# One unrolled block from the second combine to the gated layer, with other batches' stages among the heads of the masked attention

## The chip, the cores and the metric

One core of a Trainium2 chip. The metric is the device time of one execution in microseconds. Engines are named as in the profile: PE (TensorE), DVE (VectorE), ACT (ScalarE), POOL (GpSimd), SP (SyncE, which here only issues transfers).

## The reference

Two layers over x (4 batches x 512 tokens x 256), with a context of the same shape. What matters here is the second half:

```
x = x + attention_0(layernorm(x), ctx)            # 16 heads of 16, causal, relative positions
x = x + experts_0(layernorm(x))                   # 2 of 8 experts per token; the kernel's "combine" adds both
x = x + attention_1(layernorm(x), ctx, mask) @ Wo # 16 heads of 16, masked
x = x + bitlinear(silu(bitlinear(x, gate)) * bitlinear(x, up), down)
# bitlinear: each token's row scaled to +-127 and rounded, weights rounded to -1, 0, 1
```

## The kernel before, in words

A tile is 128 tokens; a batch has NI = 4 tiles, and there are 16 tiles and 64 pairs of batch and head. The kernel is a chain of blocks. In each one every engine has its own instruction stream, written out by hand; the streams meet at semaphores only, and the end of a block is a meeting of all of them. The blocks are: opening (projections), causal attention of layer 0 (unrolled), routing, the expert tiles, and then the four that the change touches:

- **combine** (L1557 ff.). For each batch SP loads the two experts' rows of its tokens (L1570, into `got`), DVE adds them to x, weighted (L1588, 8 operations a batch), takes statistics (L103), and runs the layer norm: `norm` on DVE (L111 to L125) with one square root on ACT (`root`, L149), scaling on ACT (`apply`, L143). PE turns the rows (L156), ACT copies them (L163), PE multiplies with Wq (`product`, L197, two half batches), ACT copies twice (L214, L215), and DVE splits the result in three bf16 pieces (`split`, L221 to L226), from which an f32 product is later made in one bf16 matmul over 96 rows. SP stores the pieces to DRAM (`store`, L238) and at the end waits for all of them.
- **masked_attention** (L663 ff.). A software pipeline over the 64 heads; a loop of 8 steps runs most of them (`run_heads`). At step n SP loads head n+3 (L360), PE scores head n+2 (L717) by four row blocks i, DVE takes each block's row maximum under the mask (L784, which is also what frees the bank), POOL negates the four maxima and splits them in three pieces (L758 to L766), one step later PE turns them (L731) and ACT copies them beside the head's operands (L815), so that for head n PE computes scores minus maximum, turned (L722), with the mask added by a second matmul (L724), and ACT exponentiates (L811). PE weighs the values, four heads at a time, one key block per step (`weigh`, L404); every fourth step their outputs are copied, turned and divided (`copy_out` L411, `turn` L417, `divide` L424, L426). Two banks hold scores, two the turned scores: PE waits before row block i until DVE (or ACT) has finished block i - 2. The ternary weights of the gated layer are prepared on DVE among the first and the last heads (L1653, L1673 to L1679).
- **closing** (L1002 ff.), for all batches in one pipeline: DVE copies the heads into rows of tokens (L1032), PE turns them (L1100), ACT copies (L1120), PE projects with Wo (L1107), DVE adds to x (L1041), the norm again, the largest magnitude per token (L1053), POOL scales and rounds (L1078), ACT makes bf16 integers (L1125), PE turns (L1090), ACT copies (L1129).
- **ffn** (L1682 ff.), per tile: gate and up products (L1767, L1772, two banks each), Silu on ACT (L1820), product on DVE (L1731), its maximum (L1733) and four scales (L1735 to L1740), rounding on POOL (L1751), integers on ACT (L1812), transposes (L1781), copy (L1807), down product (L1789), scaling and sum on DVE (L1717), output by SP (L1757).

```
for n in range(first, ROUND):                     # run_heads, L335: the order of every engine
    step(n, n % ROUND, n // ROUND)
...
wait(pe, s_soft, NI * m + i - 1)                  # before L717: DVE is at most two blocks behind
wait(pe, s_exp, NI * m + i - 1)                   # before L722: the same for ACT
pe.wait_ge(s_mp, 5 * (m + 1))                     # before L731: POOL's pieces of the maxima
```

## Time and profile before

| | us |
|---|---|
| median of 3 runs (1203.1 to 1204.17) | 1203.2 |
| the profiled execution, its own time | 1203.75 |
| its span | 1202.0 |
| combine (735 to 793) | 58 |
| masked attention (793 to 1087) | 294 |
| closing and gated layer (1087 to 1202) | 115 |

A span is the time from the first to the last instruction. "Busy" counts time in which an engine executes; an engine that waits for a semaphore is idle, and the profile names what released it. A granted clock of 1.00 stands for TensorE's full 2.4 GHz.

### The profile page before, as it was taken

To read this page: it belongs to the slowest core of one execution; us is meant where nothing else is said; L and a number is where in the kernel's file an instruction comes from. 1 tells how busy PE (TensorE), PEld (TensorE's weight loads), DVE (VectorE), ACT (ScalarE), POOL (GpSimd) and SP (SyncE) were. 2 spreads that over 40 slices of the span, in tenths; PEclk is the share of its full clock that TensorE was granted. 3 is DMA by queue.
4 is the path that set the end of the run, shared out by engine and by line. 5 is a ranking of instruction groups with operands and counts; after the bars stand their busy time and mean duration, and the time that the engine had idled before them with its cause. 6 is when DMAs were issued, how large, how long until landed. Compare 5 with 4: busy or idle time off the path is not lost. (4 is left out here: it accounts for less than half of the span.)

```text
span 1202.0 us, 21977 instructions
## 1 busy us (share of the span) xinstructions
PE 1050.5 (87%) x6945; PEld 658.6 (55%) x6979; DVE 659.1 (55%) x1993; ACT 636.5 (53%) x1275; POOL 200.0 (17%) x466
## 2 busy tenths in 40 slices
PE   7999999999978698999999991648999999987487
PEld 5555555655545498999999981213333333325254
DVE  4427888888856611211111104857666666775697
ACT  2447877877633232333333321526777777763697
POOL 0000000000000122222222210012222222330222
PEclk9958999999999898999999995869999999998798
DMA  5087898888749336666666644443111111100001
GB/s 184 1 306 293 321 330 322 316 321 324 290 141 360 136 110 226 223 222 219 225 218 222 220 140 153 152 147 91 47 49 46 47 46 46 47 20 10 0 32 40
DMA packets 75342, 199.55 MB, mean 166 GB/s; under 512 B 7880, under 2 KB 40904, under 8 KB 69256
## 3 DMA queue, kind: packets, MB, share of 16 engines
q1 hardware_dynamic: 71528, 188.45, 46.1%
q0 software_dynamic: 3744, 10.23, 2.2%
q8 instruction: 36, 0.59, 0.2%
q14 instruction: 34, 0.28, 0.1%
HBM read 134.82 MB, written 63.83 MB: 165 GB/s over the span
## 5 line engine op out<-in xcount | busy, mean ns | idle before, releaser
L784 DVE CUSTOM_DVE_ANT_0 unused<-mpsS,mask_bias 128x512 bf16<-128x512 f32 x256 | 172.0, 691 | 83.3 <-PE mpsS L717 82.9
L1526 ACT ACTIVATE hT<-ph,w 128x128 f32<-128x128 f32 x312 | 89.2, 369 | 207.7 <-PE ph L1500 207.7
L811 ACT ACTIVATE mPT<-mpsB 128x512 f32<-128x512 f32 x256 | 152.7, 597 | 81.1 <-PE mpsB L724 67.1
L1500 PE MATMUL ph<-xT,w 128*128 128x128 f32 x1248 | 152.1, 282 | 7.5 <-DMA w<-in_w1p 7.1
L1500 PEld LDWEIGHTS ph<-xT,w 128*128 128x128 f32 x1248 | 147.3, 197 | 10.8 <-issue 10.5
L1545 DVE TENSOR_TENSOR xn<-py,b 128x256 f32<-128x256 f32 x39 | 16.6, 425 | 247.4 <-PE py L1510 247.4
L1510 PE MATMUL py<-w,hT 128*128 x624 | 141.2, 379 | 0.7 <-DVE xn L1545 0.7
L659 ACT ACTIVATE scores<-scores,nm 128x512 f32<-128x512 f32 (+3 forms) x256 | 125.6, 557 | 9.8 <-DVE nm L624 9.8
L1510 PEld LDWEIGHTS py<-w,hT 128*128 128x128 f32 x624 | 115.6, 190 | 15.2 <-issue 1.1
L717 PE MATMUL mpsS<-mqk 96*128 96x512 bf16 x256 | 101.2, 397 | 19.5 <-DMA mqk<-packed 15.7
L611 DVE CUSTOM_DVE_ANT_0 scores<-psS,bias 128x512 f32<-128x512 f32 (+3 forms) x176 | 77.8, 487 | 54.6 <-PE psS L552 38.2
L618 DVE COPY PT<-psT 128x1024 f32<-128x1024 f32 (+1 forms) x96 | 100.2, 1044 | 7.2 <-PE psT L568 7.1
L722 PE MATMUL mpsB<-mqk 99*128 99x512 bf16 x256 | 98.9, 386 | 0.3 <-ACT mPT L811 0.2
L568 PE MATMUL psT<-ident,scores 128*128 128x128 f32 x640 | 89.7, 280 | 10.1 <-DVE PT L618 10.1
L724 PE MATMUL mpsB<-maskT,identb 128*128 128x512 bf16 x230 | 88.5, 385 | 0.0
L568 PEld LDWEIGHTS psT<-ident,scores 128*128 128x128 f32 x640 | 69.8, 143 | 18.6 <-DVE PT L618 16.8
L650 ACT COPY stage<-psE 128x1024 f32<-128x1024 f32 (+1 forms) x62 | 54.2, 874 | 46.9 <-PE psE L536 45.9
L1474 POOL DMA_INDIRECT pair_out<-xn,dst_row x39 | 42.5, 1089 | 213.7 <-DVE xn L1545 213.7
L717 PEld LDWEIGHTS mpsS<-mqk 96*128 96x128 bf16 x256 | 24.9, 98 | 85.4 <-DVE mmx L784 36.0
L404 PE MATMUL psOm<-mPT,spreadm 128*32 128x512 f32 x512 | 67.8, 604 | 1.2 <-ACT headsm L411 0.8
L390 POOL TENSOR_TENSOR spreada<-V,zerosa 128x272 f32<-128x272 f32 x16 | 11.6, 724 | 325.0 <-PE psOa L404 267.2
L546 PE MATMUL psS<-xnT,xn 16*128 16x512 f32 (+3 forms) x256 | 62.6, 508 | 0.5 <-DVE mx L611 0.5
(267 smaller groups left out, 1621.5 us busy)
## 6 DMA issues: line engine op xcount, KB each, us to landing
w<-in_w1p SPq DMA_DIRECT2D x39, 1028.0 KB, 5.8
rel<-stage SPq DMA_DIRECT2D x44, 640.0 KB, 4.6
bias<-rel SPq DMA_DIRECT2D x44, 640.0 KB, 7.1
x<-rel SPq DMA_DIRECT2D x20, 640.0 KB, 6.8
mqk<-packed SPq DMA_DIRECT2D x64, 192.0 KB
w<-in_w2p SPq DMA_DIRECT2D x8, 1024.0 KB, 12.7
rel<-x SPq DMA_DIRECT2D x10, 640.0 KB, 3.2
rel<-mask_bias SPq DMA_DIRECT2D x10, 640.0 KB, 5.0
```

The source lines that it names most:

```text
L568: tr = nc.tensor.transpose(psT[:, h, to:to + P], scores[p % 3][:, h, at:at + P], ident[:, :])
L611: ttr = nc.vector.tensor_tensor_reduce(out=scores[soft % 3][:, h, at:at + w], in0=psS[:, h, off:off + w], in1=bias[soft % 3][:, h, at:at + ...
L618: nc.vector.tensor_copy(PT[late % 4][:, :, 512 * u:512 * u + WU[u]], psT[:, :, 0:WU[u]]).then_inc(s_tev, 1)
L659: ex = nc.scalar.activation(to, to, ACT.Exp, bias=nm[:, soft % 3, h, i:i + 1], scale=1.0 / 4)
L717: nc.tensor.matmul(psS[i % 2][:, :], qk[slot][0:KP, i * P:(i + 1) * P], qk[slot][0:KP, S:2 * S], start=True, stop=True).then_inc(s_smm, 1)
L722: nc.tensor.matmul(psB[i % 2][:, :], qk[slot][:, S + i * P:S + (i + 1) * P], qk[slot][:, 0:S], start=True, stop=False)
L724: nc.tensor.matmul(psB[i % 2][:, :], identb[:, :], maskT[:, i, :], start=False, stop=True).then_inc(s_bmm, 1)
L784: nc.vector.tensor_tensor_reduce(out=unused[:, i, :], in0=psS[i % 2][:, :], in1=mask_bias[:, i, :], scale=1.0, scalar=-3.0e38, op0=ALU.add ...
L811: nc.scalar.activation(PT[r][:, j, :], psB[j % 2][:, :], ACT.Exp, scale=1.0 / 4).then_inc(s_exp, 1)
L1500: mm = nc.tensor.matmul(ph[half][:, q * P:(q + 1) * P], w1[i][:, dk * F + f * P:dk * F + (f + 1) * P], xT[i][:, dk, :], start=(dk == 0), s ...
L1510: mm = nc.tensor.matmul(py[:, 0:D], hT[i][:, f, :], w2[:, bass.ds(e, 1), f * D:(f + 1) * D].rearrange("p a d -> p (a d)"), start=(f == 0), ...
L1526: g = nc.scalar.activation(hT[i][:, f, :], ph[half][:, q * P:(q + 1) * P], ACT.Gelu, bias=w1[i][:, DK * F + f:DK * F + f + 1])
```

## The change

The four blocks become two: `masked_layer` (which holds combine of all batches, all 64 heads, and closing and gated layer of batches 0 to 2) and `final_batch` (closing and gated layer of batch 3). `PieceProjection`, `combine`, `run_heads`, `TernaryWeights`, `closing` and `ffn` go. All loops over heads are unrolled. Every engine walks over the same steps n = -16 ... 72 with four slots i each, and a few functions say what else is in a slot:

```diff
+            CLOSE, FFN = 23, 28
+            EARLY = B - 1
...
+                def combine_at(n):
+                    b, at = n // HEADS + 1, n % HEADS
+                    return (b, at) if b < B else (None, None)
+                def closing_at(n, i):
+                    c, at = divmod(NI * (n - CLOSE) + i, NI * HEADS)
+                    return (c, at) if 0 <= c < EARLY else (None, None)
+                def ffn_at(n, i):
+                    c, at = divmod(NI * (n - FFN) + i, NI * HEADS)
+                    if not 0 <= c < EARLY or at >= 5 * ROUND:
+                        return None, None, None
+                    t, k = divmod(at, ROUND)
+                    now = NI * c + t if t < NI else None
+                    return now, (NI * c + t - 1 if t > 0 else None), k
+                def weight_at(n, i):
+                    w, at = divmod(n - 2, 6)
+                    return (w, NI * at + i) if 0 <= w < 3 else (None, None)
```

So combine of batch b + 1 begins with the first head of batch b (batch 0 in the 16 steps before any head, where nothing else runs), closing of batch c at step 23 + 16 c, a tile of its gated layer every two steps from 28 + 16 c on. SP:

```diff
+                    for n in range(FIRST, last + 1):
+                        b, at = combine_at(n)
+                        if b is not None and at in (9, 10):
+                            store_queries(b, at - 9)
+                        if at == 4 and b + 1 < B:
+                            load_pairs(b + 1)
+                        if n in (-3, -2):
+                            load_weight(n + 3)
+                        if n == 7:
+                            load_weight(2)
+                        if h := head_at(n, LOAD):
+                            m, slot, turn = h
+                            if m % ROUND == 0:
+                                sp.wait_ge(s_qout[m % HEADS // ROUND], 3 * 16 * (m // HEADS + 1))
+                            wait(sp, s_bmm, NI * (m - RING + 1))
+                            load_head(sp, m, qk[slot][0:KP, :], s_qk[slot])
```

PE, behind the row block of each slot. All added products share two banks: `psU`, and `psX`, in which the heads' outputs are turned too. `u_free` and `x_free` name the semaphore that frees them:

```diff
+                            if b is not None and (at, i) in ((6, 0), (6, 2)):
...
+                                rows_turned(b, i // 2)
+                                u_free = s_tcev, DK * b + i // 2 + 1
+                            if b is not None and (at, i) in ((7, 0), (8, 2)):
+                                pe.wait_ge(*u_free)
+                                queries(b, at - 7)
+                                u_free = s_qf, DK * b + at - 7 + 1
...
+                            if c is not None and at in (0, 2):
...
+                                heads_turned(c, at // 2)
+                            if c is not None and at in (4, 6):
+                                pe.wait_ge(*x_free)
+                                projected(c, at // 2 - 2)
+                                x_free = s_res, 2 * c + at // 2 - 1
+                            if c is not None and at == 18:
+                                pe.wait_ge(*u_free)
+                                tokens_turned(c)
...
+                            if now is not None and k in (0, 4):
+                                pe.wait_ge(*u_free)
+                                wide(psU, 0, now, k // 4, s_g)
+                                u_free = s_a, 2 * now + k // 4 + 1
+                            if now is not None and k in (1, 5):
+                                pe.wait_ge(*x_free)
+                                wide(psX, 1, now, k // 4, s_u)
+                                x_free = s_h, 2 * now + k // 4 + 1
+                            if prev is not None and k == 2:
+                                pe.wait_ge(*u_free)
+                                hidden_turned(prev)
+                                u_free = s_he, prev + 1
+                            if prev is not None and k == 7:
+                                pe.wait_ge(*x_free)
+                                down(prev)
+                                x_free = s_y, prev + 1
```

The other engines follow the same table. DVE, behind the maximum of its slot: statistics of combine at step 3, the norm at (4, 0); in closing the sums at 5 and 7, statistics at 8 and 9, the norm at 10, the largest magnitude at 13, six scales at 14; in a tile's eight slots gate times (tanh + 1) at 1 and 5, hidden product at 2 and 6, maximum at 6, scales at 7, the previous tile's result at the next 0. ACT: in combine of batches 1 to 3 the eight weightings of `got` (steps 0 and 1), in a tile tanh at 0 and 4, integers of the previous tile at 1, its copy at 2. POOL: in combine of batches 1 to 3 the eight additions (steps 1 and 2), the scaling (step 5) and the splits (steps 7 to 9); in closing scaling (11, 12) and rounding (15, 16); in a tile the previous tile's rounding at 0. In a step POOL's negation of the maxima stands behind all of these.

Two computations change form. The norm has no square root on ACT any more, but a bit trick and three Newton steps on DVE (13 small operations):

```diff
+                nc.vector.tensor_scalar(self.sd[:, :].bitcast(I32), self.ve[:, :].bitcast(I32), -0.5, self.SEED,
+                                        ALU.mult, ALU.add).then_inc(self.s_rs, 1)
+                for k in range(self.ROUNDS):
...
+                    nc.vector.tensor_tensor(self.t1[:, :], self.sd[:, :], self.sd[:, :], ALU.mult).then_inc(self.s_rs, 1)
+                    nc.vector.tensor_tensor(self.t2[:, :], self.t1[:, :], self.half[:, :], ALU.mult).then_inc(self.s_rs, 1)
+                    nc.vector.scalar_tensor_tensor(out=self.sd[:, :], in0=self.t2[:, :], scalar=1.5, in1=self.sd[:, :],
+                                                   op0=ALU.add, op1=ALU.mult).then_inc(self.s_rs, 1)
```

And in batches 0 to 2 Silu is made from Tanh, while `final_batch` keeps Silu:

```diff
+                        nc.scalar.activation(hid[T % 2][:, half * S:(half + 1) * S], psU[:, :], ACT.Tanh,
+                                             scale=gh[:, T % NI:T % NI + 1]).then_inc(s_th, 1)
...
+                        nc.vector.scalar_tensor_tensor(out=part, in0=part, scalar=1.0, in1=psU[:, :],
+                                                       op0=ALU.add, op1=ALU.mult).then_inc(s_a, 1)
```

Smaller: `divide` writes the heads' outputs straight as rows of tokens, so the copies L1032 go; the query product is copied once by ACT and its first piece made by DVE or POOL; the query's buffers are single (`full`, `left`); the ternary weights are prepared in steps 2 to 19, in the room of the context (`ctxT`), no longer partly at the end. `final_batch` does closing for 4 tiles with the norm, the scaling and the rounding on DVE, and the gated layer for 4 tiles as before with two banks each.

## Rows read from the trace of the kernel before

**Rows 1.** Windows by stage: us, each engine's busy time (instructions), granted clock, DMA share, GB/s.

```profile
core 0 of [0], span 1202.0 us
...
56.00:360.00 304.00, 287.32 (x2498) 172.70 (x2499) 221.33 (x681) 209.47 (x400) 11.58 (x16) 0.93 0.80 293
...
735.00:793.00 58.00, 24.31 (x64) 11.70 (x64) 43.85 (x125) 21.44 (x44) 0.00 (x0) 0.71 0.52 171
793.00:1070.00 277.00, 264.49 (x1488) 92.09 (x1514) 191.73 (x545) 190.99 (x324) 79.33 (x331) 0.97 0.20 56
...
1087.00:1134.00 47.00, 24.82 (x128) 20.38 (x128) 29.10 (x130) 25.33 (x49) 7.73 (x16) 0.79 0.02 6
1134.00:1202.00 68.00, 54.29 (x377) 31.52 (x384) 55.37 (x129) 53.17 (x65) 17.95 (x16) 0.93 0.09 32
```

**Rows 2.** Timeline of one masked head: start, us, engine, line, operation, out<-in, [idle before <-releaser].

```profile
903.62 0.39 PE L717 MATMUL mpsS<-mqk 96*128 96x512 bf16 x1
...
903.85 0.38 PE L722 MATMUL mpsB<-mqk 99*128 99x512 bf16 x1
...
905.03 0.39 PE L731 MATMUL mpsM<-identb,mpieces 128*3 128x128 bf16 x4
...
906.58 0.69 DVE L784 CUSTOM_DVE_ANT_0 unused<-mpsS,mask_bias 128x512 bf16<-128x512 f32 x1
...
906.76 1.07 PE L404 MATMUL psOm<-mPT,spreadm 128*32 128x512 f32 x8
...
907.76 0.39 PE L717 MATMUL mpsS<-mqk 96*128 96x512 bf16 x1
...
908.75 0.21 POOL L766 TENSOR_TENSOR mpieces<-mrest,mpieces 128x4 bf16<-128x4 f32 x1
```

**Rows 3.** Timeline of TensorE, the weighting of the 31st head after the one above.

```profile
1038.89 1.07 PE L404 MATMUL psOm<-mPT,spreadm 128*32 128x512 f32 x8
```

**Rows 4.** Timeline from the first combine to the first masked matmul.

```profile
735.46 1.00 DVE L1588 SCALAR_TENSOR_TENSOR x<-got,prob,x 128x256 f32<-128x256 f32 x2 [15.79 <-DMA got<-pair_out]
...
742.19 0.16 DVE L121 TENSOR_TENSOR t2c<-t1c,vec 128x4 f32<-128x4 f32 x1
...
747.75 5.82 PE L197 MATMUL prpscq<-xnT,wcq 128*128 128x512 f32 x8 [0.67 <-ACT xnT L163]
...
788.30 3.18 SPq L360 DMA_DIRECT2D mqk<-packed  x4
...
793.04 1.01 PE L717 MATMUL mpsS<-mqk 96*128 96x512 bf16 x2 [12.50 <-DMA mqk<-packed]
```

**Rows 5.** Timeline, the weighting of the last masked head.

```profile
1078.95 1.06 PE L404 MATMUL psOm<-mPT,spreadm 128*32 128x512 f32 x8
```

**Rows 6.** Timeline of combine and closing: matmuls at the high clock.

```profile
756.25 3.67 PE L197 MATMUL prpscq<-xnT,wcq 128*128 128x512 f32 x8 [1.80 <-ACT piecescq L215]
...
771.53 1.09 PE L156 MATMUL lnpsc<-ident,xn 128*128 128x128 f32 x8 [4.42 <-ACT xn L143]
...
1100.21 3.72 PE L1107 MATMUL opo<-wo,aT 128*128 128x256 f32 x16 [0.72 <-ACT aT L1120]
```

**Rows 7.** Groups by line: busy us, mean ns | idle before, releaser.

```profile
L1733 DVE TENSOR_REDUCE ha<-hh 128x1 f32<-128x1024 f32 x16 | 19.5, 1220 | 0.6
...
L1812 ACT ACTIVATE hq<-hr,minus_magic 128x1024 bf16<-128x1024 f32 x16 | 18.4, 1148 | 2.5 <-POOL hr L1751 2.5
...
L1807 ACT COPY hqT<-ptx 128x1024 bf16<-128x1024 bf16 x16 | 16.2, 1012 | 5.7 <-PE ptx L1781 5.7
...
L811 ACT ACT_TABLE_LOAD x1 | 1.3, 1283 | 0.0
```

**Rows 8.** One line's instructions: min/median/max ns, first and last start.

```profile
L1751 POOL TENSOR_SCALAR hr<-hh,hs x16: 1122/1122/1124, 1140.5 to 1193.1; 128x1024 f32<-128x1024 f32 x16
```

**Rows 9.** Timeline of TensorE around a wait for a head's load.

```profile
811.90 0.39 PE L717 MATMUL mpsS<-mqk 96*128 96x512 bf16 x1 [1.95 <-DMA mqk<-packed]
...
813.69 0.61 PE L717 MATMUL mpsS<-mqk 96*128 96x512 bf16 x1
```

More of the change, by code:

```diff
@@ L685, in masked_attention @@
                 psM = ctx.enter_context(nc.psum_tensor("mpsM", [P, 1024], BF16))
+                psU = banks(ctx, "mpsU", 1)[0]
+                psX = vals.psX
+                psUb = psU[:, :].bitcast(BF16)
                 s_qk = [sem(f"s_mqk{r}") for r in range(RING)]
-                names = ("one", "smm", "soft", "mp", "mt", "row", "bmm", "exp", "seen")
-                s_seen_p = sem("s_mseenp")
-                s_one, s_smm, s_soft, s_mp, s_mt, s_row, s_bmm, s_exp, s_seen = (sem(f"s_m{n}") for n in names)
@@ L690, in masked_attention @@
-                block = ctx.enter_context(nc.Block())
+                names = ("one", "smm", "soft", "mp", "mt", "row", "bmm", "exp", "seen", "seenp", "const")
+                s_one, s_smm, s_soft, s_mp, s_mt, s_row, s_bmm, s_exp, s_seen, s_seen_p, s_cst = (sem(f"s_m{n}") for n in names)
+                names = ("gm", "x", "tc", "tcev", "qm", "qf", "split", "wqr", "wo")
+                s_gm, s_x, s_tc, s_tcev, s_qm, s_qf, s_split, s_wqr, s_wo = (sem(f"s_c{n}") for n in names)
+                s_got = [sem(f"s_got{b}") for b in range(B)]
@@ new lines, in queries, with total @@
+                    def queries(b, eh):
+                        pe.wait_ge(s_wqr, 16)
+                        pe.wait_ge(s_tcev, DK * (b + 1))
+                        for dk in range(DK):
+                            mm = nc.tensor.matmul(psU[:, :], wqr[:, dk, eh * P:(eh + 1) * P], xnTb[:, dk, :],
+                                                  start=(dk == 0), stop=(dk == DK - 1))
+                        mm.then_inc(s_qm, 1)
+                    def total(w):
+                        pe.wait_ge(s_cst, 2)
+                        pe.wait_ge(s_sum, w + 1)
+                        nc.tensor.matmul(psU[:, 0:1], ones[:, :], asum[:, w:w + 1], start=True, stop=True).then_inc(s_wt, 1)
@@ L713, in step @@
+                    pe.wait_ge(s_one, RING)
+                    u_free = x_free = None
+                    for n in range(FIRST, last + 1):
+                        soft, rows, late = (head_at(n, k) for k in (SOFT, ROWS, 0))
                         for i in range(NI):
                             if soft:
-                                m, slot, turn = soft
-                                wait(pe, s_soft, NI * m + i - 1)
-                                nc.tensor.matmul(psS[i % 2][:, :], qk[slot][0:KP, i * P:(i + 1) * P], qk[slot][0:KP, S:2 * S],
-                                                 start=True, stop=True).then_inc(s_smm, 1)
+                                score(soft, i)
@@ new lines, in hidden_integers, with hidden_out @@
+                    def hidden_integers(T):
+                        act.wait_ge(s_hr, T + 1)
+                        wait(act, s_ht, T)
+                        nc.scalar.activation(hq[:, :], hid[T % 2], ACT.Identity, bias=minus_magic[:, :]).then_inc(s_hq, 1)
+                    def hidden_out(T):
+                        act.wait_ge(s_ht, T + 1)
+                        wait(act, s_dn, T)
+                        nc.scalar.copy(hqT[:, :], psUb[:, :]).then_inc(s_he, 1)
+                    for n in range(FIRST, last + 1):
+                        if n % GROUP == 0 and (h := group_at(n, 2)):
@@ L988, in build @@
                             mask_bias, maskT)
+            wq = [sb(ctx, f"wq{n}", [P, 2 * F], BF16) for n in range(3)]
+            ws = sb(ctx, "ws", [P, 3])
             with nc.cleanup_on_exit():
[L990 to L995 removed]
```

1169 lines of the change are left out of this document (630 added, 539 removed).

## The prediction

> **What bounds the kernel now.** I read the split by stage first, then one head of the masked attention in order of time, then the seams on both sides of that stage.
>
> By stage [rows 1]: combine fills 58 us with TensorE busy for 24 of them, the masked heads 277 us with TensorE busy for 264, closing 47 us with 25, the gated layer 68 us with 54. The change puts three quarters of the half-empty stages among the heads of the full one. So the question is what the full one can still take.
>
> One head [rows 2]: the scoring matmul of its first row block starts at 903.62, the maxima of the next head in line are turned at 905.03, weighting starts at 906.76, and the following head's first matmul at 907.76, 4.14 us later. Every fourth head also turns its outputs; the average is (1038.89 - 906.76) / 31 = 4.26 us [rows 2, 3]. TensorE has no real gap in it: 12 matmuls of 512 columns, one every 0.22 us (903.62 to 903.85), four small transposes, and 1.0 us of weighting. VectorE ends its four maxima at 907.27 and pauses about 1.1 us until the next head's. But POOL then splits the maxima in five small steps, the last of them to 908.96, and TensorE needs them 1.41 us into the next head, at 909.17: a late fourth maximum is late on TensorE by nearly as much. **There is slack on VectorE and ScalarE as a sum, and almost none in the order of the steps.**
>
> **The change, part by part.**
>
> *Front seam.* Now the first masked matmul stands at 793.04 and the first combine at 735.46 [rows 4]. New, combine of batch 0 alone runs ahead: 8 multiply-adds of 0.5 (4 us), statistics 1.4, the normalization 2.7 (four aggregates 0.4, then 12 small operations of 0.16 as at 742.19, 0.2 with the handover), scaling 1.5: 745. Turning and copying in one bank, half by half, 4: 749. Each query product costs half of 5.82 at the low clock [rows 4], 0.6 of copy and 2.3 of splitting before the next copy may start: 759. The store, head 0's load (from 788.30 to 793.04 it takes 4.7 today) and a 1 MB weight load that SP issues ahead of it: about 768, bounds 762 and 773. **Gain 25 us.**
>
> *Back seam.* Today the last head's weighting ends at 1080.0 [rows 5] and the span at 1202.0 [rows 1]: 122 us. New: (a) The gated layer of batch 2 occupies steps 60 to 69, but the last head is step 63; its last two tiles have no heads beside them. With one bank of each kind a tile is a chain: rounding 1.12, integers 1.15, transposes 0.6, copy 1.01, gate matmul and tanh and product 2.1, the last half's product 0.7, maximum 1.22, scales 0.8 and the handovers [rows 7, 8], 9.3 us, where today a tile takes (1193.1 - 1140.5) / 15 = 3.5 [rows 8]. Two tiles and the last one's way out: 29 us. (b) The final block: closing for one batch, nothing overlapped: turns 2, projection 5.5 cold (3.72 warm [rows 6]), sum, statistics and norm 4, scaling, maxima, rounding, integers, turning 8: 19.5. Then four tiles: 68 - 12 x 3.5 = 26 [rows 1, 8], less 1 for the drain already in it: 25. Sum (a) + (b) 73.5, bounds 68 and 82. **Gain 48.5 us.**
>
> *TensorE work moved among the heads*, per batch, warm: turning for the queries 1.09, query products 3.67 [rows 6]; turning the heads 1.1, projection 3.72, tokens 0.5; four tiles of 8 x 0.22 + 0.5 + 0.9 = 3.1 each. Three batches of the first five (30 us), and ten tiles (31; two run behind the heads). TensorE is full, so all of it lengthens the stage: **+60 us.** With these three terms alone the sum would be 1203.75 - 25 - 48.5 + 60 = 1190.
>
> *New waits inside the steps.* Each engine's order is fixed, TensorE may be only two row blocks ahead of VectorE (L784) and ScalarE (L811), and psU and psX are single banks.
> - The norm (2.7 us) stands in one slot on VectorE behind the first maximum, in front of the second. TensorE's fourth block needs the second: instead of at 2.4 us it starts at 4.5. Wait 2.1, three times in combine. With ScalarE's eight extra multiplications (1.0), the splits ahead of POOL's negation (0.6) and smaller ones: 3.9 per combine, and 2.5 once where the combine of batch 3 meets the gated layer of batch 0. Together 14.
> - In closing the norm stands behind the third maximum, so the fourth, POOL's negation and the turned maxima are late (2.4). Then the largest magnitude (1.2) and six scales (1.2) in adjacent slots push the fourth maximum and POOL again (2.6); integers (1.1) and the turning of the tokens wait for POOL's rounding, which queues behind the negation (1.2); the collision with the query product in psU 0.5. Sum 6.7, three times: 20.
> - A tile of the gated layer: ScalarE's integers wait for POOL's rounding (1.12), which queues behind the negation, and TensorE's transposes wait for them: 1.2 us. The down product waits for the last product on VectorE: 0.5. So 1.8 for each of the eight tiles fully beside heads: 14.
> - Transfers: the pair loads (1 MB) and the query stores (768 KB per half batch, two) stand on SP's queue ahead of head loads that are prefetched by about one step. Today a head load in such company left TensorE idle 1.95 us before 811.90 [rows 9]. Nine such meetings against three now, some covered by the longer steps: 8.
>
> The sum is 56. Counted singly, waits that fall into one step are partly counted twice, so I take **46**, bounds 0 (the engines catch up in the weighting microsecond) and 75.
>
> *At no cost:* the weights' three magnitudes and nine roundings on VectorE run among heads today and stay there, only earlier; the masked stage pays them either way. Dividing straight into rows of tokens saves VectorE's copies of the heads, which stood beside the closing's first transposes. Unrolled code instead of a loop costs nothing: the causal block is unrolled already, and TensorE is busy for 287 of its 304 us [rows 1]; if that cover fell, it would be a wait before steps, which I leave in the upper bound. The square root on ScalarE goes (its place is taken by the small steps priced above).
>
> Sum: 1203.75 (the profiled execution: its span of 1202.0 and 1.75 around it; the median of the runs, 1203.2, is 0.5 below) - 25 - 48.5 + 60 + 46 = **1236 us**.
>
> **Rivals.**
>
> *Covered (ends faster).* The place is VectorE's pause after the fourth maximum and the microsecond of weighting: if those absorb the bursts, the waits cost at most 10 us and the time is about 1197. For: VectorE was busy 192 of 277 us and ScalarE 191 [rows 1], and the moved work raises a head with a gated tile to only about 5.3 on VectorE against 5.7 on TensorE. Against: the maxima's way over POOL has next to no slack [rows 2]. It decides at waits of 13 us in sum. Chance 0.17.
>
> *The clock falls.* After the idle 1.95 us the matmuls from 813.69 on take 0.61 instead of 0.39, the lower of the two levels (1.2 against 2.4 GHz), for about 3 us [rows 9]. Closing makes several waits of 1 to 2.4 us per batch, the tail more. If a dozen of them cost 1.7 us each, the time is 1256. Against: the masked stage as a whole was granted 0.97 [rows 1]. Chance 0.15. The Trainium skill, TensorE: Matmul & The Clock Gate, section A second HAM failure mode: psum-queue depth-cycling, says that short idles between groups which cycle through accumulation banks make the clock swing; by it this rival would be the forecast.
>
> *Tables.* The new gate uses Tanh between Exp. Every change of function set costs a load of 1283 ns on ScalarE [rows 7]. Two loads for each of the 24 gates are 61 us, 5.1 per tile, on an engine whose own work fills most of a tile's two steps: some 50 us come on top, 1286. The profile can't tell whether Tanh shares Exp's set. Chance 0.03. The Trainium skill, ScalarE: Activation LUTs, section Table sets: the hidden batching unit, lists tanh in exp's set, and the chance goes by that.
>
> **How the numbers follow.** Forecast 0.60, its own range 1214 to 1252 (waits 24 to 62); covered 0.17; clock 0.15; tables 0.03; 0.05 for anything in between that ends within 0.2% (2.4 us, about what a measurement of this kernel can tell from no change). The range 1197 to 1258 takes in the covered case and the clock, and leaves out the tables and the tails. Faster 0.17, same 0.05, slower 0.78.
>
> **What would show it.** The first masked matmul about 25 us earlier. Heads alone still 4.1 to 4.6; a pair of heads with a gated tile about 13 us instead of 8.5; between steps CLOSE + 2 and FFN about 19 us instead of 13. TensorE's idle time released by VectorE's maxima, by POOL's pieces and by ScalarE's integers. No wave of table loads. From the last head's weighting to the end 73 us. Wrong, if gated pairs take under 12 us and closing steps under 5 each: then the covered case holds; or if heads without added work have become longer, which would be the code or the loads.

## The result, and the profile after

The changed kernel takes 1248.4 us (median of 4 runs, 1246.3 to 1250.6) against 1203.35 for the kernel before in the same session: ratio 1.037, 95% interval 1.035 to 1.040. It is 3.7% slower. The profiled execution took 1249.97 us, its span is 1247.9.

Line numbers are now those of the changed kernel: L748 scores, L756 and L758 score again with keys and queries exchanged, L1004 takes VectorE's maxima, L938 to L946 are POOL's negation and pieces, L766 turns them, L1203 the exponentials, L341 the weighting. "Step n" with a time is the stretch from the weighting of step n - 1 to that of step n. Two rows of the split by stage:

```profile
core 0: us, PE busy (x) PEld busy (x) DVE busy (x) ACT busy (x) POOL busy (x), PEclk, DMA share, GB/s
769.10:802.60 33.50, 24.51 (x96) 7.38 (x100) 25.14 (x77) 18.92 (x34) 13.07 (x40) 0.81 0.27 86
802.60:1171.40 368.80, 320.60 (x1798) 127.14 (x1832) 250.18 (x723) 230.64 (x387) 146.82 (x389) 0.96 0.17 52
```

The second is the stretch from the weighting of step 4 to that of step 63. In the kernel before the same 59 steps ran from 824.61 to 1078.95 [rows 5], 254.3 us; the weighting of its step 4 and its split of that stretch:

```profile
824.61 1.06 PE L404 MATMUL psOm<-mPT,spreadm 128*32 128x512 f32 x8
...
824.60:1079.00 254.40, 247.09 (x1443) 86.45 (x1470) 177.77 (x499) 181.76 (x310) 74.54 (x304) 1.00 0.16 44
```

So the heads became 114.6 us longer: TensorE is busy 73.5 us more (320.6 against 247.1) and idle 41 us more (48.2 against 7.3), and the granted clock is 0.96 where it was 1.00. Three differences make up the whole:

| | before | after | difference |
|---|---|---|---|
| start to weighting of step 4 | 824.6 | 802.6 | -22.0 |
| step 4 to step 63 | 254.3 | 368.9 | +114.6 |
| step 63 to the end | 123.1 | 76.5 | -46.6 |

Both seams gave back nearly what was forecast. The first masked matmul, which stood at 793.04 [rows 4], stands here (timeline of the front):

```profile
756.84 4.61 SPq L713 DMA_DIRECT2D packed<-pieces  x6
761.49 0.68 SPq L706 DMA_DIRECT2D ctxT<-in_gateT  x1
762.21 0.87 SPq L299 DMA_DIRECT2D mqk<-packed  x1
...
769.11 1.04 PE L748 MATMUL mpsS<-mqk 96*128 96x512 bf16 x2 [12.63 <-DMA mqk<-packed]
```

The loss is inside the heads. The weightings of steps 22 to 27, across the first closing, and of steps 29 to 31, the first with two tiles of the gated layer under way, against 4.26 us a step on average before [rows 2, 3]:

```profile
897.94 1.07 PE L341 MATMUL psOm<-mPT,spreadm 128*32 128x512 f32 x8
905.57 1.06 PE L341 MATMUL psOm<-mPT,spreadm 128*32 128x512 f32 x8
914.87 1.06 PE L341 MATMUL psOm<-mPT,spreadm 128*32 128x512 f32 x8
919.21 1.06 PE L341 MATMUL psOm<-mPT,spreadm 128*32 128x512 f32 x8
930.06 1.41 PE L341 MATMUL psOm<-mPT,spreadm 128*32 128x512 f32 x8
936.77 1.07 PE L341 MATMUL psOm<-mPT,spreadm 128*32 128x512 f32 x8
...
946.77 1.07 PE L341 MATMUL psOm<-mPT,spreadm 128*32 128x512 f32 x8
954.67 1.06 PE L341 MATMUL psOm<-mPT,spreadm 128*32 128x512 f32 x8
961.18 1.07 PE L341 MATMUL psOm<-mPT,spreadm 128*32 128x512 f32 x8
```

Steps 23 and 24 (7.6 and 9.3 us) hold the turned heads, the projection and both query products, in the timeline four groups of 1.9 us: TensorE's own work. Step 26 takes 10.85 us and has hardly any of it. Its timeline, from the closing's normalization on:

```profile
919.58 0.38 DVE L276 BATCH_NORM_AGGREGATE mvd<-statsd 128x2 f32<-128x6 f32 x4
...
922.13 0.69 DVE L1004 CUSTOM_DVE_ANT_0 unused<-mpsS,mask_bias 128x512 bf16<-128x512 f32 x1
922.24 2.42 POOL L295 TENSOR_SCALAR xn<-x,mvd,sdd 128x256 f32<-128x256 f32 x2 [2.29 <-DVE sdd L290]
...
922.89 0.39 PE L748 MATMUL mpsS<-mqk 96*128 96x512 bf16 x1 [2.08 <-DVE mmx L1004]
...
925.93 2.42 POOL L295 TENSOR_SCALAR xn<-x,mvd,sdd 128x256 f32<-128x256 f32 x2
926.02 0.58 PE L766 MATMUL mpsM<-identb,mpieces 128*3 128x128 bf16 x4 [2.30 <-POOL mpieces L946]
926.53 0.61 PE L748 MATMUL mpsS<-mqk 96*128 96x512 bf16 x1
...
928.39 1.22 DVE L1038 TENSOR_REDUCE am<-xn 128x4 f32<-128x1024 f32 x1 [4.03 <-POOL xn L295]
929.52 0.68 DVE L1004 CUSTOM_DVE_ANT_0 unused<-mpsS,mask_bias 128x512 bf16<-128x512 f32 x1
```

Here the reader sees the chain: the norm holds a maximum back (TensorE idle 2.08 us), POOL scales two tiles before it splits the maxima (TensorE idle 2.30 us), and VectorE then stands 4.03 us in front of the largest magnitude until POOL has scaled the other two, with the step's fourth maximum queued behind it. Behind the two idles of TensorE its matmuls last 0.61 instead of 0.38 us. Steps 25 to 27 in one row:

```profile
914.87:936.77 21.90, 15.93 (x85) 5.58 (x85) 14.38 (x55) 10.16 (x17) 12.50 (x26) 0.84 0.20 64
```

The same three steps took 12.90 us before, TensorE busy for 12.84 of them at a clock of 1.00. So of the 9.0 us more, 5.9 are idle time of TensorE, and 3.1 are busy time, at a granted clock of 0.84. Over all heads the view of waits gives (TensorE's largest, and VectorE's of this kind):

```profile
PE mpsM L766 <- POOL mpieces L946: 14.8, 15, 2.3
DVE am L1038 <- POOL xn L295: 12.1, 3, 4.0
PE mpsU L827 <- ACT ctxT L1186: 9.9, 9, 1.9
PE mpsS L748 <- DVE mmx L1004: 9.7, 10, 2.2
```

### The profile page after: what moved, and what is told of

It is laid out like the page before. It is cut to its first block and busy times, and to the rows that moved or that the text cites. A ratio compares the mean times of both kernels' runs of the same rounds, so it can differ in the third digit from the quotient of the medians.

```text
span 1247.9 us, 20848 instructions
## 1 busy us (share of the span) xinstructions
PE 1065.7 (85%) x6943; PEld 657.5 (53%) x6983; DVE 660.3 (53%) x2006; ACT 616.3 (49%) x1240; POOL 259.8 (21%) x534
## 5 line engine op out<-in xcount | busy, mean ns | idle before, releaser
L1004 DVE CUSTOM_DVE_ANT_0 unused<-mpsS,mask_bias 128x512 bf16<-128x512 f32 x256 | 173.9, 689 | 114.2 <-PE mpsS L748 112.6
L1203 ACT ACTIVATE mPT<-mpsB 128x512 f32<-128x512 f32 x256 | 152.5, 597 | 119.7 <-PE mpsB L758 104.8
L748 PE MATMUL mpsS<-mqk 96*128 96x512 bf16 x256 | 103.0, 405 | 28.6 <-DMA mqk<-packed 14.3
L756 PE MATMUL mpsB<-mqk 99*128 99x512 bf16 x256 | 101.3, 396 | 1.6 <-ACT mqk L1207 1.0
L1915 POOL DMA_INDIRECT pair_out<-xn,dst_row x39 | 42.4, 1087 | 212.5 <-DVE xn L1986 212.5
L758 PE MATMUL mpsB<-maskT,identb 128*128 128x512 bf16 x220 | 86.6, 394 | 0.0
L748 PEld LDWEIGHTS mpsS<-mqk 96*128 96x128 bf16 x256 | 25.1, 99 | 109.7 <-issue 53.4
L587 ACT COPY stage<-psE 128x1024 f32<-128x1024 f32 (+1 forms) x62 | 54.1, 872 | 46.5 <-PE psE L473 45.5
L341 PE MATMUL psOm<-mPT,spreadm 128*32 128x512 f32 x512 | 72.4, 638 | 0.4
```

What stands on the lines that cost most here:

```text
L748: nc.tensor.matmul(psS[i % 2][:, :], qk[slot][0:KP, i * P:(i + 1) * P], qk[slot][0:KP, S:2 * S], start=True, stop=True).then_inc(s_smm, 1)
L756: nc.tensor.matmul(psB[i % 2][:, :], qk[slot][:, S + i * P:S + (i + 1) * P], qk[slot][:, 0:S], start=True, stop=False)
L758: nc.tensor.matmul(psB[i % 2][:, :], identb[:, :], maskT[:, i, :], start=False, stop=True).then_inc(s_bmm, 1)
L1004: nc.vector.tensor_tensor_reduce(out=unused[:, i, :], in0=psS[i % 2][:, :], in1=mask_bias[:, i, :], scale=1.0, scalar=-3.0e38, op0=ALU.add ...
L1203: nc.scalar.activation(PT[n % ROUND][:, j, :], psB[j % 2][:, :], ACT.Exp, scale=1.0 / 4).then_inc(s_exp, 1)
```

## The experiments

Ratios are to the kernel before, timed beside each run. Its median there lay between 1204.5 and 1206.8 us, against 1203.35 beside the change, so rows are best compared by their ratios. "Heads" is the stretch from the weighting of step 4 to that of step 63, "tail" from there to the end of the span, both from the one profiled execution of each. The first masked matmul stands between 766.5 and 772.1 us in runs that hardly differ up to there, so a difference of 2 us in front of the heads says nothing.

| kernel | median us | ratio, 95% interval | heads | tail |
|---|---|---|---|---|
| before | 1203.35 | | 254.3 | 123.1 |
| the change | 1248.4 | 1.037, 1.035 to 1.040 | 368.9 | 76.5 |
| e_shift | 1243.5 | 1.032, 1.028 to 1.036 | 365.0 | 73.1 |
| e_thin | 1251.1 | 1.038, 1.035 to 1.041 | 365.6 | 75.9 |
| e_early2 | 1233.3 | 1.022, 1.019 to 1.025 | 348.5 | 80.7 |
| e_early0 | 1210.3 | 1.004, 1.002 to 1.005 | 283.2 | 123.1 |
| e_order | 1242.5 | 1.032, 1.029 to 1.036 | 364.8 | 73.6 |
| e_turn | 1265.9 | 1.051, 1.048 to 1.054 | 383.3 | 73.5 |
| e_turn2 | 1247.9 | 1.036, 1.033 to 1.038 | 366.4 | 74.6 |
| e_order0 | 1203.0 | 0.999, 0.996 to 1.001 | 276.7 | 124.1 |
| e_both2 | 1235.1 | 1.024, 1.020 to 1.029 | 350.3 | 80.6 |
| e_lay2 | 1217.9 | 1.012, 1.010 to 1.014 | 332.7 | 80.6 |
| e_tern0 | 1207.8 | 1.003, 1.001 to 1.004 | 281.3 | 123.4 |
| e_late0 | 1196.5 | 0.993, 0.991 to 0.995 | 275.2 | 124.3 |

**e_shift: POOL's scaling in another form.**

```
-  ns.tensor_scalar(xn[:, t, :], x[:, t, :], self.mv[:, j, 0:1], self.sd[:, j:j + 1], ALU.subtract, ALU.mult)
+  ns.tensor_scalar(xn[:, t, :], x[:, t, :], self.sd[:, j:j + 1], self.shift[:, j:j + 1], ALU.mult, ALU.add)
```

> The changed kernel with one edit: the scaling of the normalization (the second LayerNorm's and the combine's) multiplies by 1/sigma and adds a shift, as the rounding does, in place of subtracting the mean and multiplying; VectorE computes the shift in one more small operation per batch. Theory A (POOL's scaling is slow because of its form: 1.21 to 1.30 us for 128x256 against 0.47 for the rounding of the same size, and VectorE and then the fourth maximum wait up to 4.0 us for four of them): the scaling falls to about 0.5 us, each closing loses about 3 us, each combine among heads about 2, the small operation gives 1 back: 1234 us, between 1229 and 1239. Rival B (POOL is slow there because VectorE works beside it, or because of two scalar pointers): the scaling stays above 1.1 us and the time is within 2 us of 1248. Rival C (the scaling gets faster, but steps are bound by something else in the closing): scaling 0.5 us and time above 1243.

The groups of POOL, the change first, then this run:

```profile
L295 POOL TENSOR_SCALAR xn<-x,mvc,sdc 128x256 f32<-128x256 f32 x12 | 15.5, 1304 | 0.1
L295 POOL TENSOR_SCALAR xn<-x,mvd,sdd 128x256 f32<-128x256 f32 x12 | 14.5, 1218 | 9.9 <-DVE sdd L290 9.9
```

```profile
L298 POOL TENSOR_SCALAR xn<-x,sdc,shiftc 128x256 f32<-128x256 f32 x12 | 7.5, 639 | 0.1
L298 POOL TENSOR_SCALAR xn<-x,sdd,shiftd 128x256 f32<-128x256 f32 x12 | 6.5, 553 | 10.5 <-DVE shiftd L293 10.5
```

The form is what made it slow: 0.55 us instead of 1.22 with two scalar pointers in both. But by the ratios the time fell by about 6 us, not 14, and the first closing's steps 26 and 27 only from 10.85 and 6.71 to 9.7 and 6.3. Theory A holds for the operation; for the time neither A's range (1229 to 1239) nor B's was met, and 1243.5 lies just inside C's. The scaling was one link of the chain.

**e_thin: less TensorE work in the gated layer** (half a contraction of gate and up, one of eight blocks of the down product).

```
-  for dk in range(DK):      (gate, up)        -  for f in range(FB):      (down)
+  for dk in range(1):                         +  for f in range(1):
```

> The changed kernel with part of TensorE's work among the heads left out: of the gate and up products only the first half of the contraction (one matmul of 512 columns instead of two), of the down product one of its eight blocks. What is computed for batches 0 to 2 is therefore wrong in the gated layer; order, waits, transfers and all other engines stay. Left out per tile: 4 x 0.22 + 7 x 0.11 = 1.65 us of TensorE at the high clock, ten tiles beside heads, two behind them. Theory A (the folded gated layer costs both TensorE's work and waits around it, about half of the omitted work is hidden by waits for POOL, ScalarE and VectorE): 9 us less, 1239, between 1234 and 1243. Rival B (TensorE's sum of work is the bound): 17 to 20 us less, 1229 to 1231. Rival C (a chain of waits alone sets the step): within 3 us of 1248.

Four tiles beside heads, the change first, then this run:

```profile
946.77:1002.60 55.83, 46.87 (x283) 18.73 (x288) 43.87 (x126) 39.66 (x67) 24.01 (x58) 0.97 0.13 37
```

```profile
949.03:1004.89 55.86, 43.69 (x244) 15.75 (x248) 42.58 (x124) 39.09 (x66) 23.31 (x58) 0.94 0.12 36
```

TensorE is busy 3.2 us less and the stretch is as long as before. (The 3.2 is less than the 6.6 left out; the granted clock fell from 0.97 to 0.94 beside it.) The tiles of the second batch, which have no combine beside them, say the same more cleanly: from the weighting of step 45 to that of step 53 TensorE is busy 45.5 us in the change and 41.6 here, and the stretch takes 52.2 and 51.9. That is rival C: in steps full of gated work the time does not hang on TensorE's sum. The 3 us that the heads lost lie in the two steps of each batch that hold its first tile's gate and up products and nothing else (28, 29, 44, 45, 60, 61: 5.0 us each, here 4.6) and in step 63 (5.4 and 4.6). The ratio did not change.

**e_early2 and e_early0: fewer batches among the heads.** The late batches run in two blocks written like those of the kernel before.

```
-  EARLY = B - 1                                  +  EARLY = 2        (0)
-  final_batch(identb, wq, ws)                    +  late_batches(identb, wq, ws, EARLY)
```

> The changed kernel with projection and gated layer of batches 0 and 1 among the heads (EARLY = 2 instead of 3), and those of batches 2 and 3 behind the heads in two blocks that work like the ones of the kernel before (two banks of each kind, several tiles under way). Combine stays folded as in the change. Theory A (every folded batch costs more than it saves; the last one most, since it ends in a tail): the closing steps of batch 2 (13.5 us extra) and the gated tiles of the last four heads (6) go, and the part from the last head to the end falls from 75 to about 69: 1223 us, between 1216 and 1230. Rival B (folding the early batches is free or better, only the tail of batch 2 is at fault): 1216 or less, and unfolding more batches loses time again. Rival C (folding pays per batch, the combine or the unrolled code is at fault): above 1240.

> As the kernel with EARLY = 2, but no batch's projection and gated layer run among heads (EARLY = 0): all four run behind them in pipelined blocks as in the kernel before. What is left of the change is the combine of batches 1 to 3 among the heads, the weights' loading and rounding at its new places, and the unrolled code. Theory A (the closing and gated layer among heads are what costs; the combine is about even, 24 us gained ahead of the heads against 14 of TensorE's work and about 12 of waits): 1201 us, between 1195 and 1207. Rival B (only the tail is at fault): higher than with EARLY = 2. Rival C (combine among heads or unrolled code at fault): above 1212.

Heads and tail give the price of each part. Combine alone (e_early0): heads +28.9 against before, the stretch ahead of them -21.2, tail level: 7.7 us lost by the spans, 4.4 by the medians of its session. The first two projections and gated layers: heads +65.3, tail -42.4: 23 lost, 11.5 each. The third: +20.4 and -4.2: 16 lost. So theory A's direction holds: every folded batch loses (rival B would have had e_early2 lowest). Both numbers came out 9 to 10 us high, outside their ranges. For e_early2 the heads fell as expected (20.4 for 19.5), but the tail rose from 76.5 to 80.7 where it was to fall by 6: the change's tail is a good one. For e_early0 the combine took 28.9 among heads instead of 26 and gave back 21 instead of 24. Its steps without any added work (29 to 32) take 4.1 to 4.6 us, as in the kernel before, so unrolling by itself costs nothing there.

**e_order: the same work in other slots.**

```
-  if b is not None and (at, i) == (4, 0):  lnc.norm(dve, b)
+  if b is not None and (at, i) == (4, 3):  lnc.norm(dve, b)
-  at == 10: lnd.norm    at == 13: largest    at == 14: token_scales    (POOL at 11, 12, 15, 16)
+  at == 11: lnd.norm    at == 15: largest, token_scales                (POOL at 12, 13, 16, 17)
```

> The changed kernel with the same work in other slots: the normalization of the combine goes from behind the first maximum of its step to behind the fourth, that of the closing from behind the third maximum to behind the fourth; POOL's four scalings follow one row block later; the largest magnitude and the token scales, which stood in front of the fourth maximum of step CLOSE+3, go behind it; rounding, integers and turned tokens follow one row block later. No instruction is added or taken away. Theory A (the bursts cost because a maximum is queued behind them, and POOL's pieces and TensorE behind that; behind the fourth maximum they fall into VectorE's pause and the weighting): the step of the combine's normalization loses 2.1 us, the steps CLOSE+2 to CLOSE+4 together 5 to 6 us, three times each: 1227 us, between 1221 and 1234. Rival B (the engines' sums of work are too large, a burst costs wherever it stands): within 4 us of 1248. Rival C (the scaling on POOL, 1.2 us each, is what is waited for, and it keeps its place between two heads' pieces): between 1236 and 1244.

The time, 1242.5, lies in rival C's range and above theory A's. Step 20, with the norm of batch 2's combine, fell from 6.9 to 4.2 us, as theory A has it; the first of the three (first masked matmul to the weighting of step 6) fell from 47.0 to 44.2, and step 36, where the third meets a gated tile, from 8.1 to 7.0. The closing gained little: step 26 fell to 6.2, step 27 rose from 6.7 to 9.1. Timeline of that place:

```profile
916.97 4.84 POOL L295 TENSOR_SCALAR xn<-x,mvd,sdd 128x256 f32<-128x256 f32 x4 [1.01 <-DVE sdd L290]
...
921.85 1.22 DVE L1038 TENSOR_REDUCE am<-xn 128x4 f32<-128x1024 f32 x1 [1.52 <-POOL xn L295]
```

Four slow scalings in a row (4.84 us) now hold the negation and the largest magnitude, and the scales come on top of it. Most of the wait was moved by one step. That suggests that the two cures belong together, which e_order0, e_both2 and e_lay2 try.

**e_turn and e_turn2: the transposes of the hidden tile later.** e_turn moves ScalarE's integers too, e_turn2 leaves them.

```
 e_turn:   integers k == 1 -> 2,   transposes and copy k == 2 -> 3
 e_turn2:  integers k == 1,        transposes and copy k == 2 -> 3
```

> The changed kernel, and in a tile of the gated layer ScalarE's integers, TensorE's transposes and ScalarE's copy of them stand one row block later, so that TensorE comes to the transposes about 1.5 us later than now, when ScalarE's integers are further on (now it idles 0.8 to 1.9 us there). Nothing is added or taken away. Theory A (this wait is a good part of what a tile costs, which the halved matmuls showed not to be TensorE's work): a tile's pair of heads falls from 13.0 to about 12.0, 1238 us, between 1232 and 1243. Rival B (the wait only moves, to the second gate product behind the copy in the same bank): within 4 us of 1248. Rival C: slower by 4 or more, since the copy now stands in front of the second gate product.

> The changed kernel; in a tile of the gated layer ScalarE's integers keep their place (second row block), and only TensorE's transposes and ScalarE's copy of them go one row block later, in front of a head's weighting. Theory A (TensorE waits 0.8 to 1.9 us for the integers because it comes too early; in the run that moved both, the integers stood behind ScalarE's row copy, so the wait stayed and the copy came on top): the wait goes, the copy lies beside the weighting, a pair of heads falls from 13.0 to about 12: 12 tiles, 1236 us, between 1230 and 1242. Rival B (the wait is not the bound of a tile, the second gate product's or the down product's wait takes its place): within 3 us of 1248. Rival C (like the last run, the copy delays the exponentials behind it): 1252 or more.

In e_turn the wait stayed, since the integers now stand behind the step's row copy on ScalarE:

```profile
1065.25 0.58 ACT L1207 COPY mqk<-mpsM 3x512 bf16<-3x512 bf16 x1
1065.86 1.15 ACT L1186 ACTIVATE ctxT<-ctxT,minus_magic 128x1024 bf16<-128x1024 f32 x1
...
1067.15 0.61 PE L827 MATMUL mpsU<-identb,ctxT 128*128 128x128 bf16 x8 [1.90 <-ACT ctxT L1186]
```

By the ratios it cost 16 us. In e_turn2 the wait is nearly gone, and the time stays within noise (waits of TensorE over four tiles, the change first, then e_turn2):

```profile
PE mpsU L827 <- ACT ctxT L1186: 4.9, 4, 1.9
PE mpsS L748 <- DVE mmx L1004: 0.7, 1, 0.7
```

```profile
PE mpsS L748 <- DVE mmx L1004: 3.2, 1, 3.2
...
PE mpsU L827 <- ACT ctxT L1186: 0.9, 2, 0.5
```

That is rival B: beside a combine, other waits took its place. In the second batch's four tiles, which have no combine beside them, the wait fell from 4.0 to 1.3 us with no other in its place, and the weightings of steps 45 to 53 came 50.3 instead of 52.2 us apart. So the longest wait in a view is not by itself the price of its removal: here 1.9 us of time came of 2.7 us of waits in one place, and 0.4 us of 4.0 in the other (55.4 instead of 55.8 for steps 30 to 37).

**e_order0 and e_both2: the two cures together**, without and with gated layers among heads (e_both2 with e_turn's move).

> The kernel with EARLY = 0 (combine alone among heads), the combine's normalization behind the fourth maximum, and the scaling as a multiplication and an addition. Theory A (a combine's 9.6 us among heads are 4.8 of TensorE's work and 4.8 of waits, 2.1 of them at the normalization, 0.5 to 1 at the scaling): 8 us less than the 1210 of EARLY = 0, 1202, between 1199 and 1205, so about level with the kernel before. Rival B (bursts cost wherever they stand): 1207 to 1211.

> The kernel with EARLY = 2, with the three edits together: normalizations and largest magnitude behind the fourth maximum, scaling as a multiplication and an addition, transposes of the hidden tile one row block later. By theory A: 1233 less 6 (combine) less 11 (two closings) less 8 (eight tiles) less 2: 1206, between 1199 and 1214. If it is under 1200, folding pays once the steps are laid well; rival B (sums of work): above 1225.

e_order0 is level with the kernel before; the heads lost 6.5 us against e_early0, where 8 were expected. e_both2 missed by 29 us. Its trace says where: the eight tiles (steps 30 to 37 and 46 to 53) take 116.9 us against 108.0 in e_early2, where 8 less were expected, which is 17 of the 29 and has the sign of what e_turn's move did alone; the two closings gained 3 us (steps 25 to 28 of each) where 11 were expected.

**e_lay2: two batches folded, everything in its place.** Over e_both2: transposes and integers of the hidden tile as in e_turn2, token scales behind the next fourth maximum, rounding, integers, turned tokens and the gated layer after them, and the roundings of the weights behind the fourth maximum.

> EARLY = 2 with everything laid by the theory: normalizations and largest magnitude behind the fourth maximum, token scales behind the next fourth maximum (and what follows them later, the gated layer two steps later), scaling as multiplication and addition, integers kept and transposes one row block later, the weights' roundings on VectorE behind the fourth maximum. Theory A (a folded batch costs TensorE 17.7 us and gives back 21; all above that is waits made by the order): 1233 less 8 (combine) less 5 to 6 per closing less 1.2 per tile less 3 for the weights: 1201, between 1195 and 1212. Rival B (waits move elsewhere): 1220 to 1230.

1218, not 1201; it lies between the ranges of theory A and of rival B. The closing is mended: the weightings of steps 24 to 27,

```profile
913.78 1.07 PE L344 MATMUL psOm<-mPT,spreadm 128*32 128x512 f32 x8
918.12 1.07 PE L344 MATMUL psOm<-mPT,spreadm 128*32 128x512 f32 x8
924.49 1.06 PE L344 MATMUL psOm<-mPT,spreadm 128*32 128x512 f32 x8
928.63 1.07 PE L344 MATMUL psOm<-mPT,spreadm 128*32 128x512 f32 x8
```

take 14.85 us where the change took 21.9 and heads alone take 12.9. The same three steps took 19.7 with the order alone (e_order), 20.3 with the form alone (e_shift) and 18.2 with both (e_both2), so the rest came with the token scales and what follows them. TensorE idles 1.7 us of the 14.85 instead of 6.0, and the granted clock is 1.00 instead of 0.84. (It was 1.00 in e_order's three steps too, with 5.8 us idle but no single wait above 1.9; what exactly lowers it is not settled here.) Some of the work was only moved back by a step or two, but from the weighting of step 22 to that of step 29, which holds all of the closing in both, it is still 40.8 against 48.8 us, of which about 1 is a gate and an up product that now come later. That shows the theory for the closing: the waits came of the order and of one slow operation. The gated layer is not mended (steps 46 to 55 of this run take 61.7 us, steps 44 to 53 of the change 62.2, of the kernel before 42.3), and the weights' new place costs some us, 4.6 by the next run. Folding the two batches well still costs 332.7 - 281.3 = 51.4 us among heads (both with the weights at that place) and gives back 42.8 in the tail.

**e_tern0: the weights' roundings behind the fourth maximum.**

```
-  if w is not None and at in (2 * NI + 1, 3 * NI + 1, 4 * NI + 1):  ternary(...)
+  if w is not None and at in (2 * NI + 3, 3 * NI + 3, 4 * NI + 3):  ternary(...)
```

> EARLY = 0 with normalization behind the fourth maximum, scaling as multiplication and addition, and the nine roundings of the weights (1.36 us each on VectorE) behind the fourth maximum instead of behind the second. Theory A (a burst between two maxima delays the maxima behind it by nearly its length less VectorE's slack): steps 4 to 18 fall by 0.3 us each where a rounding stands: 3 us less than the run before it, 1200, ratio to the kernel before 0.994 to 0.998. Rival B (the roundings were covered): the same as that run, 0.9986.

Slower than e_order0 by 4.6 us of heads, against both theories. Two places make up 3.4 of it. The first of each weight's passes now stands in the slot of the first combine's norm, directly behind it:

```profile
804.32 1.28 DVE L1025 TENSOR_SCALAR ctxT<-ctxT,wscale 128x2048 f32<-128x2048 f32 x1
...
806.26 0.61 PE L751 MATMUL mpsS<-mqk 96*128 96x512 bf16 x1 [2.27 <-DVE mmx L1007]
```

TensorE's wait there was 1.46 in e_order0, and steps 5 and 6 take 14.5 instead of 12.6 us. And the load of the third weight waits for the first weight's rounding, with the heads' loads behind it on SP's queue: it is issued at 817.43 instead of 811.62, and two steps on

```profile
824.05 0.39 PE L751 MATMUL mpsS<-mqk 96*128 96x512 bf16 x1 [1.39 <-DMA mqk<-packed]
```

which makes step 8 take 7.3 instead of 5.9 us. A third effect is plain in the trace but cost little. VectorE's rounding of a weight, and POOL's negation:

```profile
816.18 1.22 DVE L1031 TENSOR_SCALAR wq<-ctxT 128x2048 bf16<-128x2048 f32 x1
```

```profile
816.47 0.99 POOL L941 TENSOR_TENSOR mneg<-mmx,mminus 128x4 f32<-128x4 f32 x1 [5.11 <-DVE mmx L1007]
```

Undisturbed the negation takes 0.20 us; here 0.99, and it ends at 817.46, with the rounding at 817.40 (seven of POOL's small steps between 809 and 879 last 0.98 to 1.22). POOL stood still while VectorE rounded. But step 7, in which this falls, takes 5.9 us in both runs, and TensorE's waits for POOL's pieces are 3.6 us over all heads against 3.2.

**e_late0: the weights late.**

```
-  w, at = divmod(n - 2, 6)       loads at n in (-3, -2) and n == 7
+  w, at = divmod(n - 42, 6)      loads at n in (37, 38) and n == 47
```

> EARLY = 0 with normalization behind the fourth maximum and scaling as multiplication and addition (the run of ratio 0.9986), and the three weights loaded, summed and rounded in steps 42 to 60 instead of 2 to 20, so that the first megabyte of weights no longer stands ahead of head 0's load on SP's queue and no rounding stands among the steps that have a combine. Theory A: the first masked matmul 2 us earlier, steps 4 to 18 shorter by 5 us in sum, steps 42 to 60 longer by 3 to 4: 3 to 4 us less, 1199, ratio to the kernel before 0.994 to 0.998. Rival B (the weights cost the same wherever they stand, and head 0's load is not held up by them): ratio 0.998 to 1.001.

1196.5 us, 0.7% under the kernel before, a little more than theory A's 0.2 to 0.6%, and the best of all. The front of this run:

```profile
758.30 4.60 SPq L716 DMA_DIRECT2D packed<-pieces  x6
762.94 3.11 SPq L302 DMA_DIRECT2D mqk<-packed  x4
767.59 1.03 PE L751 MATMUL mpsS<-mqk 96*128 96x512 bf16 x2 [9.66 <-DMA mqk<-packed]
```

From the issue of head 0's load to its matmul it takes 4.65 us, as before the change [rows 4]; in the change, with a megabyte of weights ahead of it and another behind, 6.9 (762.21 to 769.11). Steps 5 to 18 take 66.7 us (e_order0: 72.45), steps 43 to 60 82.2 (77.6): the weights cost 5.8 where they were, beside a combine, and 4.6 where they are. Together with the front (the weighting of step 4 stands at 797.06 instead of 799.49) that is the 3 to 4 us expected.

## Why the prediction was right, and where it was off

Forecast 1236, measured 1248, direction and range right. By the spans of the two profiled executions the change costs 45.9 us where the four terms say 32.5. Term by term:

- *Front seam*, 25 us by the first masked matmul: 23.9, and 22.0 by the weighting of step 4. Head 0's load with the weights ahead of it takes 6.9 us and without them 4.65 (e_late0); the prediction named that load without giving it a price of its own.
- *Back seam*, 48.5: 46.6. From the end of step 63's weighting it takes 75.4 us, forecast 73.5.
- *Waits*, 46: TensorE is idle 41 us more between steps 4 and 63. In sum the term stood. Within it: loads were priced at 8 and TensorE's wait for them is 0.6; a closing's waits were priced at 6.7, and TensorE idles 6.0 in its steps 25 to 27. The combine's norm was named at 2.1; moving it (e_order) gave 2.8, 2.7 and 1.1 us.
- **The term that was too small is TensorE's time**, 60: TensorE is busy 73.5 us more (320.6 against 247.1). The sum priced all of it at the high clock. In the change, the stretches of the heads at the lower level add up to 32.7 us, and TensorE is busy for 26.7 of them. At half the clock that is at most 13 us lost (an estimate: half of 26.7), which is the excess over 60. The largest such stretches stand behind the two waits of each closing. That is also where a pair of numbers went off: 19 us forecast for the steps from CLOSE + 2 to FFN, 21.9 measured, with the waits in them no longer than forecast.
- *That all of TensorE's work lengthens the stage* was right in the closing's steps 23 and 24 and wrong in the gated layer. e_thin took some of it away, and TensorE idled longer instead. So the split in busy and idle time adds up, but is not a split by causes. A pair of heads with a gated tile was forecast at 13 and takes 6.5 + 6.5; since its sum counted all of the tile's matmuls, that number is right by luck.
- *POOL's scaling in the closing* has no term. It takes 1.22 us a tile, against 0.47 for the rounding of the same size, and VectorE waits 4.03 for it, with the fourth maximum behind. e_shift shows what makes it slow, e_lay2 that form and order together bring 21.9 to 14.85.

*Covered* fell with every gated pair at 13 us. It was to decide at 13 us of waits; TensorE idles 41 us more. *The clock falls* came true in kind and in at most two thirds of its size: 13 us at most against the rival's 20, on top of the waits and not in their place. The measured time lies between the forecast and this rival's 1256. The masked stage was granted 0.96, before 1.00 between the same steps; in e_lay2, where most of the closing's waits are gone, it was granted 0.99. The Trainium skill, TensorE: Matmul & The Clock Gate, section A second HAM failure mode: psum-queue depth-cycling, says that short idles between groups of matmuls make the clock swing. With that rule the trace agrees in kind. *Tables*: one load of a function set stands in the masked stage, at its first exponential, and 24 gates with Tanh brought none. The Trainium skill, ScalarE: Activation LUTs, section Table sets: the hidden batching unit, lists tanh in exp's set. With that the trace agrees.

What stays open: what sets the 6.5 us of a step with half a gated tile. Halving its matmuls (e_thin) left it, and taking its longest wait away (e_turn2) gave at most half a microsecond a tile; the order of all four engines together was not tried there.

## What to carry to other kernels

Before work is folded beside a full engine, compare its work on that engine with the time that it gives back: a batch's projection and gated layer has 17.7 us of TensorE work (by the prediction's prices) and gives back 21.2 (42.4 / 2), so even without one wait the gain would be 3.5. The best order tried here costs 25.7 us of heads for a batch (51.4 / 2). Fold what fills an empty seam (the combine: 14.3 us of work for 21 to 28) and leave the rest in a block with banks of its own.

A burst on an engine costs by what is queued behind it, and two bursts in one slot add up. A chain of near-equal waits gives back little until all its links are mended. Waits can also cost a second time, by the clock: look at the granted clock behind them. What has no deadline (the weights) belongs where nothing else is folded, and off the queue in front of the first load.

## What the hardware showed that was not expected

- TensorE idled 2.08 and 2.30 us in step 26, and the matmuls behind lasted 0.61 instead of 0.38. The three steps around it were granted 0.84, and 1.00 in e_lay2, where TensorE idles 1.7 us in them.
- POOL's 128x256 tensor_scalar with two scalar pointers takes 1.22 to 1.30 us as (subtract, mult) and 0.55 to 0.64 as (mult, add); its rounding of the same size, one pointer and (mult, add), 0.47.
- VectorE's 1.22 us rounding of 128x2048 stops POOL: a 128x4 negation of 0.20 us took 0.99 and ended with it (e_tern0). The Trainium skill, SBUF — State Buffer, section SBUF: two separate sides, says that VectorE's fast modes and POOL share a pair of ports under an exclusive lock that is held for a whole instruction. By that rule, the trace agrees.
